# Low-rank adapter rows: repacked once in device memory, then read per batch in 8 KB runs

## The chip, the cores and the metric

The kernel runs on one core of a Trainium2 chip. The metric is device time in microseconds (us), from the first to the last instruction plus a small part around them, as the device counts it. The times given are medians of three runs.

## What is computed

The reference is one transformer layer over 32 sequences (batches) of 32 tokens with 256 features. Each batch carries an index from 0 to 7 that picks one of eight adapters. In short:

```python
x = x + attention(conditioned(x, index, cond_weights, fside), W_qkv, b_qkv, W_out, b_out)   # 16 heads
gate = x @ Wg + (x @ Ag[index]) @ Bg[index]         # H = 1024 features, rank R = 16
up   = x @ Wu + (x @ Au[index]) @ Bu[index]
h    = silu(gate) * up
y    = h @ Wd + (h @ Ad[index]) @ Bd[index]
x    = x + ffn(y, W1, W2, W3)                        # silu(y W1) * (y W3), Hadamard transform, W2
```

What the change touches is `Bg[index]` and `Bu[index]`: for each batch, the 16 rows (rank) of its adapter's second matrix, 1024 features each for gate and for up.

## The kernel before

The kernel is written by hand, engine by engine, with explicit semaphores. Activations lie with features on the 128 partitions and the 1024 tokens along the free axis, in two halves of 16 batches (s = 0, 1). Every float32 matrix product is made of three passes: the high part of the weights times the high part of the activations (L479), times their low part (L481), and the low part of the weights times the high part (L483). Weights come as 24 blocks from one packed array in device memory, `w_stream` (128 rows of 64.5 KB): `load_weights` (L390) on the SyncE queue loads a block of 256 KB into one of three places of `raw`, ScalarE makes the high part `w_hi` (L822), and VectorE or GpSimd the low part `w_lo`.

The order of TensorE's work is written out. For the part around the change it is: conditioning and projections of the first half and of part of the second (L498, L479 to L483), attention scores of a half in two parts (`scores`, L543 for the mask and 64 small matmuls in L553), the values product (`values`, 64 small matmuls in L579), the value projection (`v`, L532 to L534), and `project`, the output projection (L479 to L483). `project(s, c, ...)` waits for the low part of the attention output, `aux_lo` (VectorE L1130), which comes after `aux_hi` (ScalarE L873), which needs the even heads (ScalarE L867) and the odd heads (VectorE L1124) out of the values' banks. Then come the adapters' first matrices (L608) and, for each eighth m of the 1024 features, `gate_up` (L479 to L483) and for pairs of them `gate_up_adapters` (L636), which multiplies by the adapter rows in `b_own`.

`b_own` holds for every batch its adapter's 16 rows, over 16 partitions, with 16 blocks (gate and up of eight m) of 128 numbers, 8 KB to a partition. There are three such buffers: `b_own[0]` for the first half, `b_own[1]` and `b_own[2]` for 8 batches each of the second. In `w_stream` the 128 rows of all adapters (row 16 * adapter + r) have, between columns `PACKED_AT[P_GU]` and `PACKED_AT[P_D0]`, 16 blocks of 384 numbers: two blocks of 128 of `Wg` or `Wu` and one of 128 of `Bg` or `Bu`. So an adapter's row is there in 16 pieces of 512 bytes.

All of this is loaded by the SyncE queue, whose program is one sequence: the first constants, three weight blocks, `matrix`, `a_in_raw`, `resid`, then `load_weights(W_OUT)` and `load_weights(W_GU)`, the batches' indices into registers, waits for the first half's scores, `load_b_own` for the first half (16 transfers at L404), a wait for the second half's scores, three weight blocks, and so on; the other two calls of `load_b_own` come later between weight blocks. `load_b_own` issues one transfer for each batch.

Of the kernel before, what the change touches and what calls it, by code (L numbers as in the profile page):

```python
# [33 lines left out]
F32 = mybir.dt.float32  # L34
# [7 lines left out]
P = 128  # L42
# [6 lines left out]
SLOTS = P // T  # L49
GROUPS = BH // SLOTS  # L50
DC = D // P
# [6 lines left out]
N, R = 8, 16  # L58
H = 1024
HC = H // P  # L60
# [24 lines left out]
PACKED_AT = [sum(PACKED[:i]) for i in range(len(PACKED))]  # L85
P_A, P_GU, P_D0, P_AD, P_D1, P_BD, P_F = 4, 5, 5 + HC, 6 + HC, 7 + HC, 8 + HC, 9 + HC
# [78 lines left out]
def build(nc, index, first, x_slots, w_stream, matrices, w2_t, x_feat, out):  # L165
    with ExitStack() as ctx:
        def sb(name, shape, dt=F32):
            return ctx.enter_context(nc.sbuf_tensor(name, shape, dt))

        def sem(name):  # L170
            return ctx.enter_context(nc.semaphore(name))
# [44 lines left out]
        b_own = [sb("b_own0", [P, 2, 2 * HC, P]), sb("b_own1", [P, 1, 2 * HC, P])]  # L216
# [45 lines left out]
        slot_of_pair = const[:, C_ODD:C_ODD + 2]  # L262
        four = const[:, C_FOUR:C_FOUR + 4]

        banks = [ctx.enter_context(nc.psum_tensor(f"bank{i}", [P, HT], F32)) for i in range(8)]

# [27 lines left out]
        a_down_raw_loaded = sem("a_down_raw_loaded")  # L295
        a_in_made = sem("a_in_made")
        a_down_made = sem("a_down_made")
        b_own_loaded = [sem(f"b_own_loaded{i}") for i in range(3)]
        b_down_loaded = sem("b_down_loaded")
        half_added = [sem(f"half_added{h}") for h in range(2)]  # L300
# [34 lines left out]
        def wait_full(eng, name, s, m):  # L335
            bank, before = TILES[name, s, m]
            eng.wait_ge(bank_full[bank], before + 1)
# [7 lines left out]
        def wait_read(eng, name, s, m):  # L345

            bank, before = TILES[name, s, m]
            eng.wait_ge(bank_free[bank], before + 1)

        def wait_weights(eng, n):  # L350

            if n <= W_V:
                eng.wait_ge(w_lo_first, n + 1)
            else:
                eng.wait_ge(w_lo_made, n - W_V)
# [15 lines left out]
        def adapter_values(engine, b0, n):  # L371

            _, values = nc.values_load_multi_w_load_instructions(
                index_i[0:1, NG + b0:NG + b0 + n], engines=[engine], min_val=0, max_val=N - 1,
                skip_runtime_bounds_check_because="an adapter's index lies in 0 to N - 1, as the reference's gather needs")
            return values
# [4 lines left out]
        @block.sync  # L381
        def _(sp):
            sp.dma_start(const[:, :], first).then_inc(const_loaded, 16)
            sp.dma_start(fs_rows[LO_ROW:BIAS_ROWS, :], first[0:N, C_FSIDE:C_FSIDE + T]).then_inc(fs_loaded, 16)

            def load_weights(n):
                if n >= STAGES:
                    wait_weights(sp, n - STAGES)
                at, runs, step = SOURCES[n]
                sp.dma_start(raw[:, n % STAGES, :].rearrange("p (a n) -> p a n", a=runs),  # L390
                             w_stream[:, at:at + runs * step].rearrange("p (a n) -> p a n", a=runs)[:, :, 0:COLS // runs])\
                  .then_inc(raw_loaded[n % STAGES], 16)

            def adapters(b0, n):

                return adapter_values(mybir.EngineType.SP, b0, n)

            def load_b_own(i, q0, adapter, b0, n):

                for b in range(b0, b0 + n):  # L400
                    at = b // SLOTS % 2 * (P // 2) + b % SLOTS * R
                    blocks = w_stream[bass.DynSlice(adapter[b] * R, R), PACKED_AT[P_GU]:PACKED_AT[P_D0]]\
                        .rearrange("r (x k) -> r x k", x=2 * HC)
                    sp.dma_start(b_own[i][at:at + R, q0 + (b - b0) // (2 * SLOTS)], blocks[:, :, DC * P:])\  # L404
                      .then_inc(b_own_loaded[i], 16)

            def load_b_down(b0, b1):
                for b in range(b0, b1):
                    if b % 8 == 0:
                        adapter = adapters(b, 8)  # L410
                    at = b // SLOTS % 2 * (P // 2) + b % SLOTS * R
                    sp.dma_start(b_down[at:at + R, b // (2 * SLOTS)],
                                 w_stream[bass.DynSlice(adapter[b % 8] * R, R), PACKED_AT[P_BD]:PACKED_AT[P_F]])\
                      .then_inc(b_down_loaded, 16)

            for n in range(STAGES):
                load_weights(n)
            sp.dma_start(matrix[:, :], matrices).then_inc(matrix_loaded, 16)
            sp.dma_start(a_in_raw.rearrange("p x n r -> p (x n r)"), w_stream[:, PACKED_AT[P_A]:PACKED_AT[P_A] + COLS])              .then_inc(a_in_raw_loaded, 16)
            sp.dma_start(resid[:, :, :], x_feat).then_inc(resid_loaded, 16)  # L420
            sp.wait_ge(index_loaded, 16)
            load_weights(W_OUT)
            load_weights(W_GU)
            first_half, second_half = adapters(0, BH), adapters(BH, BH)
            sp.wait_ge(had_made, 1)
            sp.wait_ge(ident_made, 1)
            sp.wait_ge(blk_made, HALVES)
            sp.wait_ge(xc_hi_made, DC + 1)
            wait_full(sp, "s", 0, TILES_S - 1)
            load_b_own(0, 0, first_half, 0, BH)  # L430
            wait_full(sp, "s", 1, TILES_S - 1)
            for m in range(1, 4):
                load_weights(W_GU + m)
            wait_full(sp, "z", 0, 0)
            load_weights(W_GU + 4)
            load_b_own(1, 0, second_half, 0, BH // 2)
            load_weights(W_GU + 5)
            wait_full(sp, "y", 1, TILES_Y - 1)
            sp.wait_ge(turned, HALVES * TILES_S)
            sp.dma_start(a_down_raw.rearrange("p x n r -> p (x n r)"), w_stream[:, PACKED_AT[P_AD]:PACKED_AT[P_AD] + HC * P])              .then_inc(a_down_raw_loaded, 16)  # L440
            wait_full(sp, "z", 1, 0)
            load_b_own(2, 0, second_half, BH // 2, BH // 2)
            for n in range(W_GU + 6, W_D + 3):
                load_weights(n)
            load_b_down(0, BH)
            load_weights(W_D + 3)
            load_b_down(BH, B)
            wait_read(sp, "up", 1, HC - 1)
            sp.dma_start(tmp_a[:, :, :], w2_t.rearrange("p (j n) -> p j n", j=4)).then_inc(w2_loaded, 16)
            for m in range(HC):  # L450
                load_weights(W_F + m)
            for j, (m, s, c0, c1) in enumerate(OUTS):
                sp.wait_ge(out_made, j + 1)
                sp.dma_start(out[m * P:(m + 1) * P, s * HT + c0:s * HT + c1], tmp_b[:, min(j, 3), c0:c1])\
                  .then_inc(out_stored, 16)
            sp.wait_ge(out_stored, len(OUTS) * 16)
# [3 lines left out]
        def _(pe):  # L460
# [14 lines left out]
            def both(tiles, w, xs, start, stop):  # L475

                last = []
                for ps, (x_hi, _) in zip(tiles, xs):
                    pe.matmul(ps[:, :], w[0], x_hi, start=start, stop=False)  # L479
                for ps, (_, x_lo) in zip(tiles, xs):  # L480
                    pe.matmul(ps[:, :], w[0], x_lo, start=False, stop=False)  # L481
                for ps, (x_hi, _) in zip(tiles, xs):
                    last.append(pe.matmul(ps[:, :], w[1], x_hi, start=False, stop=stop))  # L483
                return last
# [1042 lines left out]
```

## Time and profile before

| | us |
|---|---|
| median of 3 runs | 218.26 (217.13 to 218.4) |
| the profiled execution, its own time | 217.52 |
| its span, first to last instruction | 215.7 |
| TensorE (PE) busy | 209.0 (97%) |
| GpSimd busy | 104.5 (48%) |
| VectorE (DVE) busy | 96.2 (45%) |
| ScalarE (ACT) busy | 93.5 (43%) |

The profiled execution's time is 1.8 us more than its span; that part lies around the instructions. The profile names TensorE's matmuls PE and its weight loads PEld (they overlap), VectorE DVE, ScalarE ACT, GpSimd POOL and the SyncE queue SPq. In the chain of waits each row is a piece of the work that ended last, with start and length. "issue" is time in which an engine waited for nothing that the profile shows. The DMA share of a stretch is the mean busy share of the core's 16 DMA engines; it can pass 1 because the packets of one engine overlap.

### The profile page before, as it was taken

What the parts mean: (1) busy time and instruction counts of PE and PEld (TensorE: products, weight loads), DVE (VectorE), ACT (ScalarE), POOL (GpSimd) and SP (SyncE); (2) the same over time, 40 slices, a digit from 0 to 9 for tenths busy, and PEclk for the clock granted to TensorE, in tenths of its full rate; (3) what the DMA queues carried; (4) which work ended last, traced back from release to release, by engine and by line L of the source; (5) the groups of instructions that cost most, each with busy time, mean ns of one, the idle gap of its engine ahead of it and who ended that gap; (6) DMA issues with size and microseconds to landing.
All of it is one profiled execution on the core that took longest, in us unless ns stands there. A gap on an engine that the chain in (4) does not pass through costs nothing.

```text
span 215.7 us, 5107 instructions
## 1 busy us (share of the span) xinstructions
PE 209.0 (97%) x1977; PEld 167.3 (78%) x1977; DVE 96.2 (45%) x173; ACT 93.5 (43%) x162; POOL 104.5 (48%) x120
## 2 busy tenths in 40 slices
PE   7899999799999999999999999999999999999994
PEld 2567787487878788787887888788888888888894
DVE  3798998489545975210211210065942222220211
ACT  2456899446866340623532432322755554430000
POOL 4005788039693613538454349102499999441000
PEclk9999999699999999999999999999999999999999
DMA  5950099646903195031210170300111000000211
GB/s 144 393 205 3 25 145 151 81 150 143 153 0 100 50 155 143 0 104 29 74 28 18 30 310 3 97 0 0 52 41 57 2 0 3 0 0 3 97 49 49
DMA packets 16263, 16.65 MB, mean 77 GB/s; under 512 B 1776, under 2 KB 13040, under 8 KB 15984
## 3 DMA queue, kind: packets, MB, share of 16 engines
q1 hardware_dynamic: 15808, 15.26, 29.5%
q10 hardware_dynamic: 432, 1.07, 1.7%
q8 instruction: 16, 0.26, 0.5%
q14 instruction: 7, 0.06, 0.1%
HBM read 15.27 MB, written 1.05 MB: 76 GB/s over the span
## 4 chain that ended last, share of the span: by engine, by line
PE 92%; DMA 3%; DVE 2%; issue 1%; SPq 0%; ACT 0%
PE bank L479 25%; PE bank L481 23%; PE bank L483 23%; PE bank L636 8%; DMA raw<-w_stream 3%; PE bank L553 2%; PE bank L676 2%; PE bank L579 2%; PE bank L608 1%; PE bank L498 1%; PE bank L533 1%; PE bank L532 1%; PE bank L534 1%; PE bank L543 1%; DVE w_lo L1062 1%
## 5 line engine op out<-in xcount | busy, mean ns | idle before, releaser
L1375 POOL TENSOR_TENSOR h_lo<-tmp_b,h_hi 128x512 fp32r<-128x512 f32 x32 | 42.5, 1348 | 41.8 <-ACT h_hi L887 41.8
L479 PE MATMUL bank<-act_hi,w_hi 128*128 128x512 f32 x144 | 52.6, 402 | 0.1
L481 PE MATMUL bank<-act_lo,w_hi 128*128 128x512 f32 x144 | 51.0, 390 | 0.0
L483 PE MATMUL bank<-act_hi,w_lo 128*128 128x512 f32 x144 | 50.9, 390 | 0.0
L1199 DVE TENSOR_TENSOR tmp_b<-bank,tmp_a 128x512 f32<-128x512 f32 x32 | 20.8, 686 | 61.8 <-ACT tmp_a L894 35.8
L1328 POOL TENSOR_TENSOR w_lo<-raw,w_hi 128x512 fp32r<-128x512 f32 x21 | 26.8, 1290 | 19.7 <-ACT w_hi L822 19.7
L479 PEld LDWEIGHTS bank<-act_hi,w_hi 128*128 128x128 f32 x144 | 27.0, 188 | 7.8 <-issue 0.8
L894 ACT ACTIVATE tmp_a<-bank 128x512 f32<-128x512 f32 x32 | 17.3, 592 | 34.8 <-PE bank L636 30.6
L483 PEld LDWEIGHTS bank<-act_hi,w_lo 128*128 128x128 f32 x144 | 27.0, 188 | 5.8
L481 PEld LDWEIGHTS bank<-act_lo,w_hi 128*128 128x128 f32 x144 | 27.1, 188 | 5.1
L887 ACT ACTIVATE h_hi<-tmp_b 128x512 fp32r<-128x512 f32 x32 | 19.7, 632 | 19.9 <-DVE tmp_b L1199 19.9
L479 PE MATMUL bank<-h_hi,w_hi 128*128 128x512 f32 (+1 forms) x72 | 22.8, 371 | 0.0
L481 PE MATMUL bank<-h_lo,w_hi 128*128 128x512 f32 (+1 forms) x72 | 22.5, 366 | 0.0
L483 PE MATMUL bank<-h_hi,w_lo 128*128 128x512 f32 (+1 forms) x72 | 22.4, 366 | 0.0
L822 ACT ACTIVATE w_hi<-raw 128x512 fp32r<-128x512 f32 x24 | 14.5, 620 | 7.0 <-DMA raw<-w_stream 6.1
L636 PE MATMUL bank<-z_slots,b_own 64*128 64x128 f32 x256 | 16.4, 278 | 0.0
L636 PEld LDWEIGHTS bank<-z_slots,b_own 64*128 64x128 f32 x256 | 14.9, 188 | 1.5 <-issue 1.1
L481 PEld LDWEIGHTS bank<-h_lo,w_hi 128*128 128x128 f32 x72 | 13.6, 189 | 2.3
L483 PEld LDWEIGHTS bank<-h_hi,w_lo 128*128 128x128 f32 x72 | 13.6, 189 | 2.2
L479 PEld LDWEIGHTS bank<-h_hi,w_hi 128*128 128x128 f32 x72 | 13.3, 189 | 2.4
L1354 POOL COPY a_in<-a_in_raw 128x64 f32 x32 | 6.6, 250 | 13.5 <-DVE w_hi L1055 12.7
L1362 POOL TENSOR_TENSOR prob<-prob,row_inv 128x512 f32<-128x512 f32 x8 | 8.6, 1088 | 7.4 <-DVE row_inv L1113 7.2
(96 smaller groups left out, 249.8 us busy)
## 6 DMA issues: line engine op xcount, KB each, us to landing
raw<-w_stream SPq DMA_DIRECT2D x24, 256.0 KB, 3.8
b_own<-w_stream SPq DMA_DIRECT2D x32, 128.0 KB, 4.4
k_x<-x_slots ACTq DMA_DIRECT2D x2, 512.0 KB, 6.2
resid<-x_feat SPq DMA_DIRECT2D x1, 1024.0 KB, 8.1
tmp_a<-w_t SPq DMA_DIRECT2D x1, 1024.0 KB, 5.0
out_feat<-tmp_b SPq DMA_DIRECT2D x3, 256.0 KB, 2.1
a_down_raw<-w_stream SPq DMA_DIRECT2D x1, 512.0 KB, 4.3
b_down<-w_stream SPq DMA_DIRECT2D x32, 16.0 KB, 1.6
```

The source lines that it names most:

```text
L479: pe.matmul(ps[:, :], w[0], x_hi, start=start, stop=False)
L481: pe.matmul(ps[:, :], w[0], x_lo, start=False, stop=False)
L483: last.append(pe.matmul(ps[:, :], w[1], x_hi, start=False, stop=stop))
L636: ins = pe.matmul(tile(name, s, m)[:, at:at + P], weight(name, s, m, rows_, q), slots(name, s, rows_, q).rearrange("p e n -> p (e n)"), st ...
L822: act.activation(w_hi[:, at:at + COLS], raw[:, n % STAGES, :], ACT.Copy)\
L887: act.activation(dst, tmp_b[:, ORDINAL[name, s, m] % 4, :], ACT.Copy).then_inc(prod_hi_made, 1)
L894: free(act.activation(tmp_a[:, n % 4, :], tile(name, s, m)[:, :], ACT.Silu), name, s, m)
L1199: free(dve.tensor_tensor(tmp_b[:, ORDINAL[name, s, m] % 4, :], tile(name, s, m)[:, :], tmp_a[:, silus % 4, :], ALU.mult), name, s, m)
L1328: pool.tensor_tensor(w_lo[:, at:at + COLS], raw[:, n % STAGES, :], f32(w_hi[:, at:at + COLS]), ALU.subtract).then_inc(w_lo_made, 1)
L1354: last = pool.tensor_copy(a_in[:, s, :, 4 * i + b, :], a_in_raw[:, :, bass.DynSlice(adapter[b], 1), :] .rearrange("p x n r -> p x (n r)"))
L1362: pool.tensor_tensor(prob[s][:, i], prob[s][:, i], row_inv[:, s, i, :].unsqueeze(2) .to_broadcast([P, 16, T]), ALU.mult).then_inc(normed, 1)
L1375: pool.tensor_tensor(lo, tmp_b[:, n % 4, :], f32(hi), ALU.subtract).then_inc(prod_split, 1)
```

## The change

A tensor `b_rows` of 128 rows by 2048 numbers (8 KB to a row, 1 MB in all) is declared in device memory. Behind `load_weights(W_GU)` SyncE issues one transfer that copies into it, from `w_stream`, the 16 pieces of 512 bytes of each of the 128 adapter rows, side by side. Before the first `load_b_own`, SyncE waits for the semaphore `b_rows_made` of that transfer. `load_b_own` then reads, for each batch, its 16 rows from `b_rows`, each one run of 8 KB, into the same place as before.

```diff
@@ declarations
+        b_rows = nc.dram_tensor("b_rows", (P, 2 * HC * P), F32).ap()
...
+        b_rows_made = sem("b_rows_made")
@@ load_b_own
                 for b in range(b0, b0 + n):
                     at = b // SLOTS % 2 * (P // 2) + b % SLOTS * R
-                    blocks = w_stream[bass.DynSlice(adapter[b] * R, R), PACKED_AT[P_GU]:PACKED_AT[P_D0]]\
-                        .rearrange("r (x k) -> r x k", x=2 * HC)
-                    sp.dma_start(b_own[i][at:at + R, q0 + (b - b0) // (2 * SLOTS)], blocks[:, :, DC * P:])\
-                      .then_inc(b_own_loaded[i], 16)
+                    sp.dma_start(b_own[i][at:at + R, q0 + (b - b0) // (2 * SLOTS)].rearrange("r x k -> r (x k)"),
+                                 b_rows[bass.DynSlice(adapter[b] * R, R), :]).then_inc(b_own_loaded[i], 16)
@@ SyncE's program
             load_weights(W_OUT)
             load_weights(W_GU)
+            sp.dma_start(b_rows.rearrange("p (x k) -> p x k", k=P),
+                         w_stream[:, PACKED_AT[P_GU]:PACKED_AT[P_D0]].rearrange("p (x k) -> p x k", x=2 * HC)
+                         [:, :, DC * P:]).then_inc(b_rows_made, 16)
             first_half, second_half = adapters(0, BH), adapters(BH, BH)
...
             wait_full(sp, "s", 0, TILES_S - 1)
+            sp.wait_ge(b_rows_made, 16)
             load_b_own(0, 0, first_half, 0, BH)
```

Only SyncE's sequence differs. On the SyncE queue before, from the last early weight blocks to the first adapter rows (a TENSOR_LOAD reads indices into registers, an ISA row is register arithmetic):

```order
L390 DMA raw<-w_stream 128x512 [waits w_lo_first,index_loaded]
L390 DMA raw<-w_stream 128x2x256 [waits w_lo_first]
L373 TENSOR_LOAD index_i x2
L404 ISA [waits xc_hi_made,blk_made,bank_full4,ident_made,had_made]
L404 DMA b_own<-w_stream 16x16x128
L404 ISA
L404 DMA b_own<-w_stream 16x16x128
```

The same stretch of the SyncE queue in the changed kernel, whose lines are numbered one to five higher:

```order
L393 DMA raw<-w_stream 128x512 [waits w_lo_first,index_loaded]
L393 DMA raw<-w_stream 128x2x256 [waits w_lo_first]
L425 DMA b_rows<-w_stream 2048x1x128
L376 TENSOR_LOAD index_i x2
L405 ISA [waits xc_hi_made,bank_full4,blk_made,b_rows_made,ident_made,had_made]
L405 DMA b_own<-b_rows 16x2048
L405 ISA
L405 DMA b_own<-b_rows 16x2048
```

One row is new, the transfer of 2048 pieces of 128 numbers. The first adapter transfer waits for one semaphore more, and each adapter transfer is 16 runs of 2048 numbers instead of 16 times 16 runs of 128. Their number and places in the queue are the same.

## Rows read from the trace of the kernel before

**Rows 1.** The page: busy time, share of the span, instructions of each engine.

```profile
PE 209.0 (97%) x1977; PEld 167.3 (78%) x1977; DVE 96.2 (45%) x173; ACT 93.5 (43%) x162; POOL 104.5 (48%) x120
```

**Rows 2.** Chain that ended last, 37 to 43 us: start, length, what.

```profile
37.29 2.06 issue
39.35 0.41 PE bank L579 x5
39.76 0.53 PE bank L543 x2
40.29 1.89 PE bank L553 x64
42.18 0.72 PE bank L479
```

**Rows 3.** The same chain, 30 to 34 us.

```profile
30.89 0.32 PE bank L543 x2
31.21 1.09 PE bank L553 x64
32.29 0.95 PE bank L579 x63
33.24 0.43 PE bank L479
```

**Rows 4.** A stretch, PE: length, busy (instructions), granted clock, DMA share, GB/s.

```profile
40.22:42.10 1.88, 1.88 (x66) 0.50 0.20 32
```

**Rows 5.** Instruction queue: over the span, then 18 to 20, then 36 to 38 us.

```profile
q8 instruction: 16, 0.26, 0.5%
...
q8 instruction: 1, 0.02, 3.1%
...
q8 instruction: 1, 0.02, 4.9%
```

**Rows 6.** Stretches from the start, instructions of PE and of PEld in brackets.

```profile
0.00:18.40 18.40, 16.43 (x127) 10.01 (x131) 13.27 (x24) 8.45 (x13) 2.64 (x12) 1.00 0.64 218
0.00:25.80 25.80, 23.83 (x223) 15.26 (x224) 20.32 (x36) 13.24 (x21) 9.09 (x40) 1.00 0.46 156
0.00:32.40 32.40, 30.43 (x345) 21.06 (x353) 26.42 (x47) 19.05 (x31) 14.17 (x45) 1.00 0.53 152
0.00:37.29 37.29, 35.32 (x462) 25.11 (x463) 30.26 (x54) 23.94 (x39) 18.18 (x49) 1.00 0.62 153
```

**Rows 7.** Stretches again; the last two numbers: DMA share, GB/s.

```profile
28.00:29.00 1.00, 1.00 (x6) 0.82 (x5) 0.97 (x3) 1.00 (x3) 0.86 (x1) 1.00 0.83 222
32.00:34.00 2.00, 2.00 (x89) 1.63 (x71) 1.71 (x4) 2.00 (x5) 1.12 (x2) 1.00 1.24 148
124.50:125.50 1.00, 1.00 (x6) 0.83 (x5) 0.32 (x1) 0.00 (x0) 0.41 (x1) 1.00 1.03 434
```

**Rows 8.** The page's DMA issues: size, median us from issue to landing.

```profile
raw<-w_stream SPq DMA_DIRECT2D x24, 256.0 KB, 3.8
b_own<-w_stream SPq DMA_DIRECT2D x32, 128.0 KB, 4.4
```

**Rows 9.** Timeline of the SyncE queue: start, length, what.

```profile
9.74 2.66 SPq L390 DMA_DIRECT2D raw<-w_stream  x2
25.35 9.13 SPq L404 DMA_DIRECT2D b_own<-w_stream  x16
```

**Rows 10.** Timeline of VectorE, then of ScalarE.

```profile
36.79 1.81 DVE L1130 SCALAR_TENSOR_TENSOR aux_lo<-q_t,const,aux_hi 128x512 fp32r<-128x512 f32 x1 [0.75 <-ACT aux_hi L873]
38.53 0.47 DVE L1124 SCALAR_TENSOR_TENSOR q_t<-bank,const,q_t 128x256 f32<-128x256 f32 x1
...
42.82 0.74 DVE L1130 SCALAR_TENSOR_TENSOR aux_lo<-q_t,const,aux_hi 128x512 fp32r<-128x512 f32 x1
...
40.89 0.72 ACT L873 ACTIVATE aux_hi<-q_t,const 128x512 fp32r<-128x512 f32 x1
```

**Rows 11.** The chain: the first use of the adapter rows.

```profile
53.76 1.99 PE bank L636 x32
```

## The prediction

> **What bounds the kernel now.** I read the page's engine line first, then the chain of waits, then the DMA queues by stretch. TensorE is busy 209.0 us of a span of 215.7 [rows 1], and the chain is its matmuls nearly throughout. The first use of the adapter rows is at 53.76 us [rows 11]; the sixteen transfers for it are issued from 25.35 on for 9.13 us [rows 9], with a median of 4.4 us to landing [rows 8]. They are there more than ten microseconds early. So faster transfers for their own sake are worth nothing. What matters is what they do to others.
>
> One piece of the chain speaks of that. At 37.29 us, in the middle of 64 small matmuls of L579, TensorE stops for 2.06 us with the label "issue": no semaphore holds it [rows 2]. A sequencer that stops in the middle of a run with no wait may have no instructions. The queue q8 brings 16 packets of 0.26 MB in all, 16 KB each [rows 5]. Narrowing the stretch of that view places three of them at 18.4, 25.8 and 36.2 us. Adding PE and PEld, TensorE has done 258 instructions by 18.4 us, 447 by 25.8, 698 by 32.4 and 925 when it stops at 37.29 [rows 6]. From 447 to 925 are 478, twice 239. I read that as: q8 is TensorE's program, a block is about 240 recorded instructions, one block is asked for each time another is begun, and TensorE runs dry if it is not there when the one in hand ends. By this the block asked for at 25.8 us + 239 instructions (686), so at about 32.4 us, was served only at 36.2 and TensorE went on at 39.35. At 18.4 us with idle DMA engines the packet took 3.1% of 2 us times 16 engines, 1.0 us; at 36.2 us 4.9%, 1.6 us [rows 5].
>
> What stood before it is the adapter rows. From 32 to 34 us the 16 DMA engines are at 1.24 with only 148 GB/s [rows 7]. SyncE issues 128 KB each 9.13 / 16 = 0.57 us, 230 GB/s [rows 8, 9], so a backlog grows. 2.1 MB at 148 GB/s take 14.2 us and reach to 40 us. The stop lies under that.
>
> The Trainium skill ("Runtime: NRT & Kernel Launch", Instruction fetch mechanics) says that programs stream in blocks of 16 KiB, 256 instructions, over a DMA queue of the sequencer's own, and that a block boundary's cost is mostly hidden. The trace agrees with the block, and at 37.29 us not with the hiding.
>
> **What the stop costs.** The 2.06 us, and then slower matmuls: from 40.22 to 42.10 us the granted clock is 0.50, which is 1.2 of 2.4 GHz [rows 4]. Each piece against its like at full clock [rows 2, 3]: five of L579 take 0.41 where 63 take 0.95, so 0.08; L543 0.53 against 0.32; L553 1.89 against 1.09; the first L479 0.72 against 0.43. That is 0.33 + 0.21 + 0.80 + 0.29 = 1.63 us, and the stop in all 3.7 us.
>
> **The change part by part.**
>
> *Adapter transfers.* Still 32, in the same queue places, with the same issue pace, I take it (0.57 us each). In place of 256 pieces of 512 bytes each has 16 runs of 8 KB. No row shows 8 KB runs onto 16 partitions. The slow bound is the present 148 GB/s. The fast bound is 434 GB/s, 8 KB rows onto 128 partitions at 124.5 us [rows 7]. At 28 us, with few transfers queued, the same 16 partitions took 222 GB/s even in small pieces [rows 7]. So the partitions as such allow about the pace of issue, and what is slow is many small pieces in the queues. I take 230 GB/s, the pace of issue: no backlog, and the block asked for at 32.4 us finds short queues. It has to start by 37.29 - (39.35 - 36.2) = 34.1 us. That saves 3.7 us. At 148 GB/s it saves nothing.
>
> The Trainium skill ("SBUF — State Buffer", Door 1: The DMA port swizzle) speaks against this: 16 neighbouring partitions reach 4 of the 16 ports. By its 435 GB/s for 16 that would be about 109 GB/s for one such transfer, however long the runs. The trace disagrees in size, with 222 GB/s at 28 us, though two transfers in flight may have used different ports. By this rule nothing is gained and the time is that of the first rival below.
>
> *The copy.* One issue, under 1 us on SyncE, which is free until 25.35 us. The transfers ahead of it are issued by 12.40 us [rows 9] and land by about 3.8 us later [rows 8], so it runs from some 15 us. It moves 1.05 MB in 2048 pieces. Bounds: 434 GB/s gives 2.4 us; half of 148, because both sides are now in device memory and in small pieces, gives 14.2 us [rows 7]. I take 148, the nearest row for such pieces: 7.1 us, to about 22 us. Nothing else wants the DMA engines then, except the instruction block of 18.4 us. That one has until instruction 447 at 25.8 us [rows 6], so 7.4 us; the block under saturation took from 32.4 to 39.35, 6.95 us. It fits by 0.4 us. Cost 0, and the cover is thin.
>
> *The wait on b_rows_made.* Behind it on SyncE are the adapter transfers and then the weight blocks. With the copy landed by 22 to 24 us it has passed before 25.35. Cost 0. Adapter rows have over ten microseconds before 53.76.
>
> *What is late next.* With the stop gone the values' product ends at 37.4, the mask and scores (0.32 + 1.09) at 38.8, and six matmuls of `project` (0.43 and five of some 0.23) at 40.4 us. The next needs the second `aux_lo`. VectorE is held by the first one until 38.6 [rows 10]; then come two odd heads of 0.47, `aux_hi` of 0.72 on ScalarE and `aux_lo` of 0.74 [rows 10]: 38.6 + 0.4 + 0.4 + 0.8 + 0.75 = 41.0 us. TensorE waits 0.6 us there. Later waits hang on TensorE's own results and move with it.
>
> **The sum.** 3.7 - 0.6 = 3.1 us, from the profiled execution's 217.5 to 214.4. The median of the runs shown is 218.26, 0.7 above the profiled one. Taking 3.1 to 3.3 off it I forecast 215.0 us. The likeliest case's own range is 213.4 (all of 3.7 and a little, off 217.5) to 216.5. A measurement of this kernel can tell about 1% from no change, which is 216.1 to 220.4.
>
> **Rivals.**
>
> 1. *The stop stays, because 8 KB runs onto 16 partitions are not faster.* At 148 GB/s, of the 230 issued from 25.4 to 32.4 us, (230 - 148) x 7 = 0.57 MB are still queued, 3.9 us; the block starts at 36.3 as now. For it: the destination is the same 16 partitions, and the slowdown of before appears only when many transfers are queued, so 28 us need not tell of it. Against: 222 GB/s at 28 us [rows 7]. Time 218.3, perhaps 219.
>
> 2. *The stop moves to 25.8 us.* The copy's own small pieces keep the block of 18.4 us waiting somewhat longer than the 7.4 us it has. With the copy at some 110 GB/s, 9.3 us instead of 6.95 means a stop of 1.9 us and a slow clock after it of about 1.6: 215.0 + 3.5 = 218.5. For it: a margin of 0.4 us only. Against: the copy is half the size of the first adapter load and ends by 22 us, which frees the queue.
>
> 3. *Slower: the copy is slow.* Reading and writing device memory in 512-byte pieces at 60 GB/s takes 17 us. The block's wait before it starts, 36.2 - 32.4 = 3.8 us, grows by 148 / 60 to 9.4; it starts at 27.8, TensorE goes on 3.15 us later at 30.95, so it stands 5.2 us from 25.8 and loses 1.6 to the clock. 215.0 + 6.8 = 221.8, and SyncE also starts the adapter rows at 32 us. It decides against the change (220.4) from a copy below about 75 GB/s, at the very end of my bounds. For it: no transfer within device memory is in the trace. Against: only that reading alone runs at 148.
>
> **How the numbers follow.** Forecast 0.52, first rival 0.23, second 0.12, third 0.13. Faster by over 1%: the forecast's 0.52 and a little of the second, 0.54. Within 1%: the first, most of the second and some of the third, 0.33. Slower: 0.13. The range goes from 213.4, below which I leave 0.08, to 219.6, which takes in the first two rivals and leaves the third's 0.12.
>
> **What would show it.** Right: no "issue" piece near 37 us in the chain, a granted clock of 1.00 from 39 to 43 us, a DMA share well under 1 from 29 to 35 us at about 230 GB/s, and a wait of TensorE of about 0.6 us on `aux_lo` near 40.5 us. The copy would show as a stretch of full DMA engines from 15 to 22 us. Wrong: "issue" pieces at 25.8 or still at 37 us, a DMA share over 1 beyond 35 us, SyncE waiting on the copy past 25.35 us. If the stop is gone and the time is not less, then my reading of what follows it is wrong.

## The result and the profile after

| | before | changed |
|---|---|---|
| median of 8 runs, us | 218.08 (216.72 to 220.32) | 219.73 (218.97 to 221.04) |
| profiled execution, us | 217.52 | 219.98 |
| its span, us | 215.7 | 218.2 |
| its mean granted clock | 0.992 | 0.984 |

The medians lie 1.6 us apart; the ratio, which leaves out the one slow execution of before (220.32), is 1.0089, with a 95% interval of 1.0052 to 1.0126. So the changed kernel is slower, where I had forecast 3.1 us faster. The first rival had the mechanism, but took the rate as unchanged; it said 218.3, perhaps 219.

The chain that ended last in the changed kernel, in the place of [rows 2] (start, length, what; L584 is the values product, L548 and L558 the mask and scores, L484 and L486 the projection):

```profile
36.40 1.04 PE bank L584 x59
37.44 3.15 issue
40.59 0.64 PE bank L584 x5
41.23 0.54 PE bank L548 x2
41.77 1.89 PE bank L558 x64
43.66 0.72 PE bank L484
44.38 0.43 PE bank L486
...
46.52 0.27 PE bank L484
```

The stop is still there, after the same 59 matmuls of 64, and lasts 3.15 us instead of 2.06. The slow clock after it lasts longer too. Over this stretch the columns are length, TensorE busy (instructions), granted clock, DMA share and GB/s:

```profile
39.50:46.50 7.00, 5.91 (x78) 0.51 0.51 108
```

The clock stands at its lower level, 1.2 GHz, from about 39.6 to about 46.4 us; before it did so from about 39.7 to 43.2. Compared piece by piece with the same work at full clock, as in the prediction but to the end of the slow stretch, that costs 2.9 us here and 1.8 before. Stop and clock make 6.1 us against 3.9. That is 2.2 of the 2.5 us between the two spans. The stop also begins 0.15 us later than before; the rest lies behind it.

The DMA engines in stretches, for [rows 7] (length, granted clock, DMA share, GB/s):

```profile
28.00:30.00 2.00, 1.00 0.88 197
30.00:32.00 2.00, 1.00 1.00 131
32.00:34.00 2.00, 1.00 1.00 131
34.00:36.00 2.00, 1.00 1.07 139
36.00:38.00 2.00, 1.00 1.14 152
```

The new transfers run at 131 GB/s, below the 148 of before. The queue's row for 32 to 34 us has 64 packets, 32 of 8 KB and 32 small ones. So on average each of the 16 engines moves one run of 8 KB in a microsecond, and is busy all of it.

```profile
q1 hardware_dynamic: 64, 0.26, 100.5%
```

TensorE's instruction block, which started at 36.2 us before, starts at 37.4 us here, and takes 5.1% of 2 us times 16 engines, 1.6 us, about as in [rows 5]:

```profile
q8 instruction: 1, 0.02, 5.1%
```

The copy, on the other hand, was fast. From the page, and from the DMA view of 15 to 18 us, which holds 0.93 MB of it:

```profile
b_rows<-w_stream SPq DMA_DIRECT2D x1, 1024.0 KB, 6.6
...
q1 hardware_dynamic: 1834, 0.93, 104.6%
```

That is 311 GB/s in 512-byte pieces, both ends in device memory. It was issued at 12.59 us and had landed by 19.2, long before the first adapter transfer at 25.5.

**What single executions show.** The executions of the kernel before fall into three groups by their mean granted clock. Of 31 timed beside the first four experiments, 8 had 1.0 (216.0 to 216.8 us), 13 had 0.99 (217.1 to 219.0) and 10 had 0.98 (219.2 to 220.3). Of the 8 of the changed kernel none had 1.0; four had 0.99 (218.97 to 219.48) and four 0.98 (219.98 to 221.04). So one kernel's time goes with whether, and how long, the clock falls behind the stop. Inside one group the changed kernel's median is 0.9 to 1.2 us above that of before, which fits the 1.1 us by which its stop is longer. The rest comes from the mix of the groups. Eight executions alone could be chance, but with the ten of the run that alternates the batches (below), which has a stop of 3.5 us, it is none of 18 with 1.0, against 8 of 31.

### The profile page after: what moved, and what is told of

Read it like the earlier page. It is cut to its first block, busy times and chain, and to the rows that moved or that the text cites. A ratio compares the mean times of both kernels' runs of the same rounds, so it can differ in the third digit from the quotient of the medians.

```text
span 218.2 us, 5109 instructions
## 1 busy us (share of the span) xinstructions
PE 210.1 (96%) x1977; PEld 167.9 (77%) x1977; DVE 97.0 (44%) x173; ACT 93.1 (43%) x162; POOL 104.5 (48%) x120
## 4 chain that ended last, share of the span: by engine, by line
PE 92%; DMA 3%; DVE 2%; issue 2%; SPq 0%; ACT 0%
PE bank L484 25%; PE bank L486 23%; PE bank L488 23%; PE bank L641 8%; DMA raw<-w_stream 3%; PE bank L558 2%; PE bank L584 2%; PE bank L681 2%; PE bank L613 1%; PE bank L503 1%; PE bank L538 1%; PE bank L539 1%; PE bank L537 1%; PE bank L548 1%; DVE w_lo L1067 1%
## 5 line engine op out<-in xcount | busy, mean ns | idle before, releaser
L484 PE MATMUL bank<-act_hi,w_hi 128*128 128x512 f32 x144 | 52.6, 402 | 0.3 <-DVE w_lo L1067 0.3
L486 PE MATMUL bank<-act_lo,w_hi 128*128 128x512 f32 x144 | 51.1, 391 | 0.0
L484 PEld LDWEIGHTS bank<-act_hi,w_hi 128*128 128x128 f32 x144 | 27.0, 188 | 7.9 <-issue 0.8
L899 ACT ACTIVATE tmp_a<-bank 128x512 f32<-128x512 f32 x32 | 17.3, 592 | 36.2 <-PE bank L641 32.0
L486 PEld LDWEIGHTS bank<-act_lo,w_hi 128*128 128x128 f32 x144 | 27.1, 188 | 5.1
L484 PE MATMUL bank<-h_hi,w_hi 128*128 128x512 f32 (+1 forms) x72 | 22.8, 370 | 0.0
L486 PE MATMUL bank<-h_lo,w_hi 128*128 128x512 f32 (+1 forms) x72 | 22.4, 366 | 0.0
L486 PEld LDWEIGHTS bank<-h_lo,w_hi 128*128 128x128 f32 x72 | 13.6, 189 | 2.3
L484 PEld LDWEIGHTS bank<-h_hi,w_hi 128*128 128x128 f32 x72 | 13.3, 189 | 2.3
```

The costliest lines, as they stand in the source:

```text
L899: free(act.activation(tmp_a[:, n % 4, :], tile(name, s, m)[:, :], ACT.Silu), name, s, m)
```

## The experiments

**Is it the copy?** The kernel before, with copy and wait, but nobody reads the copy:

```diff
+            sp.dma_start(b_rows..., w_stream[...][:, :, DC * P:]).then_inc(b_rows_made, 16)
...
+            sp.wait_ge(b_rows_made, 16)
             load_b_own(0, 0, first_half, 0, BH)     # unchanged, from w_stream
```

> The kernel before, with the copy and its wait added; the adapter rows are still read from w_stream in pieces of 512 bytes, and b_rows is read by nobody. It asks which part of the change costs the time. Theory P (the rate of the adapter transfers is set by their 16 destination partitions, and what costs is their backlog in front of TensorE's instruction blocks): the copy is done by 19 us and harmless, so the time is that of the kernel before, 218, with an issue stop of about 2.1 us near 37 us. Rival C (the copy itself shifts or delays something): the time is that of the changed kernel, 219 to 220, with a stop of about 3 us.

Measured: 218.18 us against 218.13 of before, ratio 0.9987 (0.9925 to 1.0048). The copy costs nothing that these executions can tell, which is about 1 us. Its profiled execution is one of those in which the clock did not fall:

```profile
36.68 1.04 PE bank L586 x59
37.71 1.76 issue
39.48 0.41 PE bank L586 x5
39.89 0.32 PE bank L550 x2
40.21 1.09 PE bank L560 x64
```

The same stop, and behind it mask and scores in 0.32 and 1.09 us, their full-clock lengths. Its time was 216.3 us.

**Which end of the transfers is slow?** Seven runs. In the first, each transfer of the changed kernel carries its 128 KB to all 128 partitions, 1 KB to each:

```diff
-    sp.dma_start(b_own[i][at:at + R, ...], b_rows[bass.DynSlice(adapter[b] * R, R), :])
+    x = 2 * ((b - b0) % 8)
+    sp.dma_start(b_own[i][:, ..., x:x + 2], b_rows[:, bass.DynSlice(adapter[b] * R, 2 * P)])
```

> The changed kernel, but each of the 32 adapter transfers carries the same 128 KB to all 128 partitions, 1 KB to each, in place of 8 KB to each of 16. Number, sizes, issue pace and source tensor stay. It leaves out the gather: the rows are not those of the batch's adapter. Theory P: the backlog is gone, over 220 GB/s while they are issued, the last lands by 36 us instead of 41, no issue stop near 37 us, time 214.5 to 215.5. Rival S (reading from device memory is what is slow): the DMA share stays at 1 or more with about 150 GB/s and the stop stays, 218 to 220.

Measured: 216.72 us, ratio 0.9945 (0.9884 to 1.0006). In the profiled execution the stop near 37 us was gone (one of 0.6 us stood at 61 us instead). Five executions took 215.2 to 215.8; the other five took 217.7 to 220.5 with a mean clock of 0.984 to 0.992. The rate did not fit:

```profile
32.00:34.00 2.00, 1.00 0.93 160
```

I had overlooked that 16 * adapter numbers is an offset of 64 bytes times the adapter. The same run with offsets in multiples of 1 KB:

```diff
-    b_rows[:, bass.DynSlice(adapter[b] * R, 2 * P)]
+    b_rows[:, bass.DynSlice(adapter[b] * (2 * P), 2 * P)]
```

> The earlier run with 1 KB to each of 128 partitions, but each read at a multiple of 1 KB in a row of b_rows instead of a multiple of 64 bytes. It leaves out the gather, as that one did. That run moved only 150 GB/s at a DMA share of 0.97 with all 128 partitions taking part, against theory P. If the odd offsets made that, the share falls to about 0.6 at the 230 GB/s of issue; if rows 8 KB apart or the 1 KB pieces did, it stays near 0.95.

Its stretches, with the same columns as above:

```profile
30.00:32.00 2.00, 1.00 0.77 229
32.00:34.00 2.00, 1.00 0.84 258
```

258 GB/s at a share of 0.84 in the same two microseconds, no issue stop, 214.99 us in its one execution. With the odd offsets nearly full engines moved 160, though the pieces were still 1 KB. The offsets of 64 to 448 bytes are the likely reason. They also made the adapters' pieces overlap in the source, which was not tried apart.

Next, the order of the batches, so that consecutive transfers alternate between lower and upper 64 partitions:

```diff
-    for b in range(b0, b0 + n):
+    for b in [b0 + 8 * e + c + 4 * a for e in range(n // 8) for c in range(4) for a in range(2)]:
```

> The changed kernel with the 8 batches of each group issued in the order 0, 4, 1, 5, 2, 6, 3, 7, so that consecutive transfers go to the lower and the upper 64 partitions in turn; bytes, runs and count are the same. Theory P in the form that the ports behind neighbouring partitions bind: four instead of two groups of ports take part in any four transfers, the rate rises from 131 to 200 GB/s or more, and the stop near 37 us shrinks below 1 us or goes, time 214.5 to 216. If the limit is one transfer at a time (each engine writes one partition), or lies at the source, the rate stays 131 to 150 and so does the stop, 219 to 220.

> The kernel before with the same order of batches, 0, 4, 1, 5, 2, 6, 3, 7, and no copy. Theory P as ports: 148 GB/s rises towards 220, the stop shrinks or goes, time 214.5 to 216.5. If the 512-byte pieces or the source bind here: 218, stop of 2 us as before.

Measured: 220.07 us (ratio 1.0106, 1.0059 to 1.0153) and 218.41 us (0.9988, 0.9928 to 1.0047). No gain in either. In the changed kernel the rate is the same to the digit:

```profile
30.00:32.00 2.00, 1.00 1.01 131
```

```diff
-    at = b // SLOTS % 2 * (P // 2) + b % SLOTS * R
-    sp.dma_start(b_own[i][at:at + R, ...
+    at = b // SLOTS % 2 * (P // 2) + b % SLOTS // 2 * (2 * R) + b % 2
+    sp.dma_start(b_own[i][at:at + 2 * R - 1:2, ...
```

> The changed kernel, but each adapter transfer writes its 16 runs of 8 KB to every second partition of 32 instead of to 16 neighbouring ones; source, runs, count and order are the same. It leaves out the order in which the rest of the kernel expects the rows, so each row meets the wrong coefficient. Theory P (what stands behind groups of four neighbouring partitions sets the rate, 131 GB/s for four such groups): eight groups take part, so 131 doubles to 262 and the pace of issue, 230, binds; no backlog, the engines are free by 36 us, no issue stop near 37, execution times 215 to 216 and the granted clock 1.0 in most of them. Rival S (the source or the length of a run sets 131): still 131 GB/s at a DMA share of 1.0, a stop of 3 us, 219 to 220.

> The same layout of every second partition in the kernel before, with 16 pieces of 512 bytes to a partition and no copy; rows meet the wrong coefficients here too. Theory P: the pieces were never the limit, 148 rises to 200 GB/s or more, the stop goes or shrinks, 215 to 216.5. Rival: 512-byte pieces are a limit of their own, the rate stays near 150 to 180 and the stop near 1 to 2 us, 217 to 218.

Measured: 214.74 us (ratio 0.9875, 0.9799 to 0.9951) and 214.77 us (0.9885, 0.9807 to 0.9962), with all eight executions within 1 us. The stretches of the first and then of the second:

```profile
30.00:32.00 2.00, 1.00 0.68 193
32.00:34.00 2.00, 1.00 0.67 176
```

```profile
30.00:32.00 2.00, 1.00 0.61 168
32.00:34.00 2.00, 1.00 0.67 161
```

With runs of 8 KB, 131 GB/s at a full share became 193 at 0.68; with pieces of 512 bytes, 148 at 1.24 became 168 at 0.61. It is tempting to divide rate by share and call that twice the speed. The two experiments further below that hold back SyncE forbid it. They write the same neighbouring partitions in the same pieces as before, with only four or three transfers in flight. Over 27 to 37 us, first the kernel before, then four in flight, then three:

```profile
27.00:37.00 10.00, 1.00 1.06 148
27.00:37.00 10.00, 1.00 0.79 130
27.00:37.00 10.00, 1.00 0.50 128
```

And every second partition, first with runs of 8 KB, then with pieces of 512 bytes:

```profile
27.00:37.00 10.00, 1.00 0.55 154
27.00:37.00 10.00, 1.00 0.51 137
```

Three in flight to neighbouring partitions have nearly the rate and the share of every second partition in pieces. So the share falls with the depth of the queue as well, and the quotient tells two placements apart only when both have full engines. The queue was shorter with every second partition too, because SyncE now issued a transfer only each 0.8 to 1.0 us instead of each 0.57 (12.97 and 15.32 us for sixteen).

For 8 KB runs the partitions are shown to matter all the same. Sixteen transfers in 12.97 us are 162 GB/s, more than the 131 at which neighbouring partitions have full engines, and yet the share is only 0.55 and the transfers land in 2.9 us. For pieces of 512 bytes they are not: the pace of 15.32 us is 137 GB/s, less than the 148 of before, so the slower issue alone could have kept the queue short. The run with 128 partitions and even offsets has a pace of 10.00 / 16 = 0.63 us, and there the stop is gone as well. No run put neighbouring and every second partition at one pace, so how much of the gain is the slower issue stays open.

The source, last, in a single execution: runs of 8 KB read from `w_stream` instead of `b_rows`.

```diff
-    b_rows[bass.DynSlice(adapter[b] * R, R), :]
+    w_stream[bass.DynSlice(adapter[b] * R, R), PACKED_AT[P_GU]:PACKED_AT[P_GU] + 2 * HC * P]
```

> The changed kernel, reading its 16 runs of 8 KB from w_stream itself (8 KB in one run from each row, which are the wrong numbers) instead of from b_rows; the copy is still made. One look at the rate. Theory P: the source does not matter, 131 GB/s at a DMA share of 1.0 from 30 to 34 us. Rival S (b_rows, rows of 8 KB side by side, is a slow place to read from): over 180 GB/s.

```profile
30.00:32.00 2.00, 1.00 0.98 139
32.00:34.00 2.00, 1.00 1.01 143
```

139 to 143 GB/s at a full share, and a stop of 2.33 us; the execution took 216.16 us, and its clock did not fall. The source matters by a tenth at most.

**Does the block wait for what is queued?** The kernel before, rate and places as they were, but SyncE holds back:

```diff
+    if b - b0 >= 3:
+        sp.wait_ge(b_own_loaded[i][(b - b0) % 3], 16 * ((b - b0) // 3))
```

> The kernel before, with SyncE waiting before each adapter transfer until the third last one has landed (three semaphores in turn instead of one). Rate, bytes and places are the same, only the number queued at a time falls from about eight to three. Theory Q (the instruction block waits in proportion to what is queued when it is asked for): the stop near 37 us falls below 0.5 us or goes, 215 to 216.5. If it is the mere business of the DMA engines that delays the block, whatever the depth, the stop stays at 2 us or more and the time at 218 or, as the loading lasts longer, above.

> As the run with three transfers in flight, but with four. With three the stop was gone, and the weight blocks behind them in SyncE's queue were issued at 42.7 us instead of about 39.5 and became late. With four the sixteen transfers should take about 14 us, to 39.5 us. Theory Q (the block waits for what is queued): no stop or one under 1 us, weight blocks nearly in time, 215 to 217. If four in flight are already as many as the engines hold at their slow rate, the stop is back at 1 to 2 us and the time at 217 to 218.5.

The block starts at 34.1 us with three in flight and at 34.0 with four, instead of 36.2. With four the engines were nearly full all the same:

```profile
30.00:32.00 2.00, 1.00 1.03 137
32.00:34.00 2.00, 1.00 0.90 137
```

So it is what is queued, and not the mere business of the engines, that delays the block. In both the stop of L579's 64 matmuls is gone and the mean granted clock is 0.999 or 1.0 in all 20 executions. That much of the theory holds. The time did not follow: 218.26 us (ratio 1.0029, 0.9986 to 1.0071) with three, a miss, and 217.05 us (0.9962, 0.9923 to 1.0000) with four. With three, the chain shows a part of why:

```profile
38.39 3.74 DMA b_own<-w_stream
...
42.71 3.21 DMA raw<-w_stream
45.94 0.64 ACT w_hi L826
...
46.65 2.56 POOL w_lo L1332 x2
49.22 1.00 POOL k_x L1372
50.22 1.24 POOL w_lo L1332
```

SyncE is held by its adapter transfers until 42.62 us. So the weight blocks behind them come no earlier than before (42.3 us), while they can be issued at 39.3 us when SyncE is free (the kernel before with the layout below). GpSimd's sequence hangs on them, and TensorE waits for it 0.6 us, until 60.86 us. Four in flight mend most of that, but a second new wait is in both. The stops of the adapters' matmuls, with more semaphores to wait for ahead of each group, come to 1.1 us in three places with three in flight, and to 1.8 us in four places with four (L638, "issue"):

```profile
PE bank L638 <- issue: 1.8, 4, 0.6
```

That these come from the added waits is my reading; it was not tried by itself.

**A version that beats both.** Every second partition, with nothing left out: `a_in`'s 32 columns for a pair of batches are stored in the order (rank, batch) instead of (batch, rank), and the mask of the z rows picks the batch by partition parity.

```diff
-        a_in = sb("a_in", [P, HALVES, 2 * DC, BH, R])
+        a_in = sb("a_in", [P, HALVES, 2 * DC, BH // 2, R, 2])
...
-    pool.tensor_copy(a_in[:, s, :, 4 * i + b, :],
+    pool.tensor_copy(a_in[:, s, :, 2 * i + b // 2, :, b % 2],
...
+    f[:, C_MIX:C_MIX + SLOTS] = (2 * (p // T % 2) + p % 2)[:, None] == np.arange(SLOTS)
```

> The kernel before with every adapter row in every second partition, now with the rest made to fit (a_in's columns and the masks of the z rows in the same order), so that nothing is left out; no copy. Theory P from the two runs with this layout (214.7 and 214.8): 214.5 to 215.5, the granted clock 1.0 in nearly every execution, no issue stop near 37 us, a wait of 0.8 us on aux_lo. If writing a_in in steps of two costs GpSimd or the weight loads something: up to 1 us more.

> The changed kernel (copy, runs of 8 KB) with the same fitted layout of every second partition. It asks what the copy is worth once the partitions no longer bind. Theory P: nothing, as the loads are hidden either way: within 0.5 us of the run with this layout and no copy. If long runs do help then (fewer packets in the way of the instruction blocks), 0.5 us or more faster than it; if the copy disturbs the start, as much slower.

Measured: 214.93 us without the copy (ratio 0.9884, 0.9836 to 0.9931) and 214.88 with it (0.9876, 0.9812 to 0.9940). GpSimd's copy into `a_in` takes 242 ns instead of 236, the weight loads 110 ns as before. The copy in device memory is worth nothing here either, and costs nothing: the two medians differ by 0.05 us. The profile without it has these waits of TensorE, and no others:

```profile
PE bank L690 <- DVE warm L1019: 1.2, 1, 1.2
PE bank L481 <- DVE aux_lo L1132: 0.8, 1, 0.8
PE bank L500 <- DVE prob L1048: 0.3, 1, 0.3
```

## Why the prediction was wrong, point by point

- *What bounds the kernel, and the stop at 37.29 us.* Right. In all six runs with the stop, TensorE goes on 3.0 to 3.2 us after the block on q8 has started: started at 36.2 the stop is 2.06 us, at 36.9 it is 2.60, at 37.4 it is 3.15. Started at 34.1 or before there is none; nor is there one in the first run with 128 partitions, where it started at 34.9 but took only 1.0 us instead of 1.6. By the prediction's count the block is asked for at 31.9 to 32.8 us. Even with light queues it starts only at 32.9 to 33.8, so about 1 us of the delay was never backlog, but it fits before the limit of 34.1 that the prediction worked out.

- *What the stop costs.* 3.7 us forecast, 3.9 when summed to the end of the slow clock. But I took this from one execution. The clock does not fall behind every stop (it stayed at 1.00 in the profile with the copy alone), and in the changed kernel's it stays low about twice as long, 6.8 us against 3.4.

- *Adapter transfers, "I take 230 GB/s".* This is the step that failed. It measured 131, so the term of 3.7 us saved became 2.2 us lost. I had the bound of 148 and the first rival beside it, and went past them on one row: 222 GB/s from 28 to 29 us. I put the slowness down to many small pieces in the queues; with few long runs in their place it was a little worse, 131 against 148. That row is the start of the load, with few transfers queued, and the changed kernel has the like of it (197 at 28 to 30 us) just before it falls to 131. A rate at a DMA share below 1 while queues fill does not tell what holds when they are full. The bound at the slow end was also too high: nothing in the rows excluded a rate under 148, and the first rival should have had a stop longer than before.

- *The Trainium skill against the row.* The rule that I weighed and set aside ("SBUF — State Buffer", Door 1: The DMA port swizzle) fits the runs in its structure. By it 16 neighbouring partitions reach 4 ports and every second of 32 reaches 8. Here 131 GB/s at full engines became 162 over thirteen microseconds, with engines that were not full; a full load on every second partition, which would show a doubling, was not run. Its figure, 109 for four ports, lies below the 131 measured; the measurement decides. The same page (Can I just issue two DMAs to hit both halves?) says that separate transfers do not combine to reach more ports, and in the alternating order the rate stayed at 131.

- *The copy.* Cost 0 was right, as far as the runs can tell. Its rate was mis-sized, 148 taken and 311 measured, because I took the slow rate for one of small pieces. The copy itself shows that small pieces are not the limit: it has the same 512 bytes, at full engines, and twice the rate. The second and third rivals, which lived on a slow copy, fell with that.

- *The wait on b_rows_made.* Right, passed long before.

- *What is late next.* Right where the stop is gone: TensorE waits 0.8 us on `aux_lo`, forecast 0.6, and goes on at 40.85 us, forecast 41.0. The gain of 3.1 us is there too, 217.5 to 214.5 in the profiled executions without the copy, but it came with every second partition and not with the runs of 8 KB. That the stop's price was forecast so closely is partly luck, since against the executions of before in which the clock does not fall, with a median of 216.24 us, the gain is only 1.3 us.

- *Why 8 KB runs are slower than pieces, 131 against 148.* Not settled. The source may have a part in it, as 8 KB runs read from `w_stream` took 139 to 143.
## What to carry to other kernels

A transfer that is hidden can still cost time, by what is queued in front of an engine's instruction block; look for "issue" pieces in the middle of a run of like matmuls, and for many transfers in flight at that time. Before changing the source or the piece length of a slow transfer, ask how many partitions it writes, and compare its rate with that of another transfer with pieces as short, both at full engines: a rate taken while the queues are short tells of neither. Here moving 16 rows from neighbouring partitions to every second one gave 1.2%. Repacking the source cost 0.9% with the old placement and gave nothing with the new one.

## What the runs showed of the hardware that I had not expected

- Pieces of 512 bytes between two places in device memory moved at 311 GB/s, twice the rate of the same pieces into 16 partitions.
- Reading 1 KB pieces at offsets of 0 to 448 bytes in steps of 64 took the engines 0.93 of their time for 160 GB/s; at multiples of 1 KB, 0.84 for 258.
- The DMA share is no fixed price per byte: with the same pieces and partitions, 148 GB/s stood at a share of 1.24 with SyncE issuing freely, 137 at 1.03 with four transfers in flight, and 132 at 0.51 with three.
- SyncE issued a transfer each 0.57 us to neighbouring partitions and only each 0.8 to 1.0 us to every second partition.
- A stop of 1.8 to 3.5 us is followed by a granted clock of 0.5 in some executions and not in others of the same kernel; over 31 executions that spread the time from 216.0 to 220.3 us.
